# When layer 1's expert weights and row scatters are sent: 13 experts moved into attention rounds 7 and 8

## The reference

```python
x = x + L0_attn(layernorm(x))     # 16 heads of 16, RMS norm of q and k, rotary, causal softmax
x = x + L0_moe(layernorm(x))      # 16 experts, top 2, one shared expert
x = x + L1_attn(layernorm(x))     # 16 query heads, one key/value head, xpos rotary, causal softmax
x = x + L1_moe(layernorm(x))      # 32 experts in 8 groups, top 4 groups, top 8 experts, shared expert
```

## Time and profile before

| | us |
|---|---|
| median of 3 runs | 1161.76 |
| lowest and highest | 1159.61, 1175.99 |
| the profiled execution's own time | 1172.08 |
| its span | 1169.5 |
| TensorE busy, GpSimd busy in the span | 899.2 (77%), 621.2 (53%) |

### The profile page before, as it was taken

How to read it: one execution, slowest core, us unless ns; L and a number is a source line. 1 busy time by engine, 2 the same in 40 slices (tenths; PEclk the granted TensorE clock), 3 DMA queues, 4 the chain that set the end, 5 groups by cost and what they waited for, 6 DMA issues and landing times.

```text
span 1169.5 us, 22075 instructions
## 1 busy us (share of the span) xinstructions
PE 899.2 (77%) x5927; PEld 691.8 (59%) x5927; DVE 685.6 (59%) x2692; ACT 467.1 (40%) x1176; POOL 621.2 (53%) x870
## 2 busy tenths in 40 slices
PE   1687989878597992379987888856899999989900
PEld 1465667657355881256665565533688887778700
DVE  4678888865532554467687674352455544444568
ACT  2346666743112441257655443311344444444400
POOL 3646666523163652336558888755356655545500
PEclk9859999988798996559989576787999999999955
DMA  8500000000624543400002222566455655545287
GB/s 231 192 2 1 2 2 1 1 2 1 263 106 127 152 130 120 144 1 2 2 29 86 85 97 101 210 222 221 147 163 174 182 157 161 153 141 156 70 327 319
DMA packets 73093, 136.97 MB, mean 117 GB/s; under 512 B 13406, under 2 KB 51725, under 8 KB 70928
## 3 DMA queue, kind: packets, MB, share of 16 engines
q1 hardware_dynamic: 52144, 85.15, 22.8%
q0 software_dynamic: 17632, 46.73, 11.2%
q10 hardware_dynamic: 3200, 3.70, 0.9%
HBM read 79.15 MB, written 62.39 MB: 121 GB/s over the span
## 4 chain that ended last, share of the span: by engine, by line
PE 36%; DVE 9%; POOL 6%; issue 5%; ACT 2%; another core or an unknown queue 1%; DMA 1%; DVEq 0%; POOLq 0%; ACTq 0%; SPq 0%
PE s_psum L1996 12%; PE s_psum L2009 6%; PE s_psum L1988 3%; POOL rows L1553 3%; PE s_psum L1477 3%; PE s_psum L2004 2%; DVE a_masked L1074 2%; DVE f_rows L2096 2%; DVE f_xT L2096 2%; PE s_psum L549 1%; POOL a_probs L1414 1%; PE s_psum L1496 1%; PE s_psum L646 1%; PE s_psum L602 1%
## 5 line engine op out<-in xcount | busy, mean ns | idle before, releaser
L2106 POOL DMA_INDIRECT parts<-e_y,e_dest x206 | 202.7, 984 | 180.7 <-DVE e_y L2079 96.9
L1996 PE MATMUL s_psum<-wres,e_xT 128*128 x824 | 213.9, 382 | 1.8 <-ACT e_xT L2036 1.0
L1996 PEld LDWEIGHTS s_psum<-wres,e_xT 128*128 128x128 f32 x824 | 156.1, 191 | 26.1 <-issue 5.4
L1414 POOL TENSOR_SCALAR_AFFINE_SELECT a_probs<-a_probs 128x256 f32<-128x256 f32 x256 | 107.5, 444 | 117.6 <-ACT a_probs L870 116.8
L1553 POOL DMA_INDIRECT rows<-f_rows,f_place_at x128 | 125.2, 978 | 40.3 <-issue 31.7
L2009 PE MATMUL s_psum<-wres,e_hT 128*128 x412 | 125.3, 386 | 12.2 <-ACT e_hT L2046 11.6
L870 ACT ACTIVATE a_probs<-s_psum 128x768 f32<-128x768 f32 x128 | 104.6, 817 | 72.8 <-PE s_psum L629 68.2
L2041 ACT ACTIVATE e_act_out<-s_psum 128x128 f32<-128x128 f32 x206 | 57.1, 277 | 180.8 <-PE s_psum L1996 101.6
L2070 DVE TENSOR_TENSOR e_hid<-e_act_out,s_psum 128x128 f32<-128x128 f32 x206 | 59.0, 286 | 91.8 <-issue 42.6
L1074 DVE CUSTOM_DVE_ANT_0 a_masked<-s_psum,a_ahead 128x128 f32<-128x128 f32 (+1 forms) x256 | 76.1, 353 | 42.0 <-PE s_psum L605 39.1
L2079 DVE TENSOR_SCALAR e_y<-s_psum,e_xg 128x256 f32<-128x256 f32 x206 | 99.6, 484 | 0.7 <-issue 0.7
(11 more groups left out here) (297 smaller groups left out, 1993.4 us busy)
## 6 DMA issues: line engine op xcount, KB each, us to landing
e_xg<-rows SPq DMA_DIRECT2D x159, 160.0 KB
f_rows<-parts SPq DMA_DIRECT2D x8, 1024.0 KB, 7.2
f_xT<-parts SPq DMA_DIRECT2D x8, 1024.0 KB, 7.4
wres<-in_experts SPq DMA_DIRECT2D x21, 384.0 KB
e_xg<-rows SPq DMA_DIRECT2D x47, 144.0 KB
wres<-in_experts SPq DMA_DIRECT2D x4, 1536.0 KB
rows<-empty SPq DMA_DIRECT2D x1, 5120.0 KB, 24.1
e_yk<-parts SPq DMA_DIRECT2D x16, 256.0 KB, 2.9
```

The source lines that it names most:

```text
L1414: last = nc.gpsimd.affine_select(out=diagonal[:, :, a], in_=diagonal[:, :, a], compare_op=ALU.is_ge, fill=0.0, base=0, pattern=[[0, 2], [1 ...
L1996: last = nc.tensor.matmul(ps_u[b % 2][:, 0:2 * P], xT[b % 2][:, c * P:(c + 1) * P], wres[:, ds(e, 1), 2 * c * P:2 * (c + 1) * P].rearrange ...
L2106: nc.gpsimd.indirect_dma_start(out=parts[:, :], out_offset=bass.IndirectOffsetOnAxis(ap=dest[b % NY][:], axis=0), in_=y[b % NY][:], in_off ...
```

## The change

Experts 25 to 13 are sent in rounds 7 and 8: GpSimd's queue adds 1 to `paced` in each of the 13 steps from round 7 step 0 to round 8 step 4. The other 13 are sent one per four scatters from round 9 on (counts 76, 80, ...). SyncE waits for what still uses the memory: `group_ps` (the last stack transposed) ahead of the first, batch 5's shifted scores ahead of expert 18, batch 6's ahead of expert 15, batch 7's and the last maxima ahead of expert 12, the last placement ahead of expert 4. Experts 4 to 0 are single transfers too. In steps 0, 1 and 2 of round 9 and step 0 of round 10 there is one scatter instead of two, so 118 are sent in the loop and 10 in `finish`. Some buffers of the attention are allocated in another order, so that those in use longest lie under the lowest experts.

```diff
-PACED = 78
+STACK_EXPERTS, FIRST_QUERY_EXPERTS, SECOND_QUERY_EXPERTS = 19, 16, 13
+ROUND_STEPS = 13
+PACE = 4
...
+        pieces = NH // 2 + (NK // 2 if multi else 1)
+
+        def query_homes(i):
+            return (sb(f"qT{i}", [P, PAIRS, N], F32R), sb(f"kT{i}", [P, PAIRS if multi else 1, N], F32R))
+
+        ahead = sb("ahead", [P, TRI])
+        masked = wide("masked", [P, 2, 2, TRI])
+        max_stack = sb("max_stack", [P, TB, 2, 2 * NH, 2], F32R)
+        maxT = sb("maxT", [P, TRI], F32R)
+        pairs_by_age = {i: query_homes(i) for i in (1, 0, 2)}
+        qT, kT = ([pairs_by_age[i][n] for i in range(NQ)] for n in range(2))
...
-                sp.wait_ge(st_ps, PAIRS * B)
-                sp.wait_ge(max_done, PAIRS * B)
-                for n, e in enumerate(range(FREE_EXPERTS - 1, LAST_EXPERTS - 1, -1)):
+                sp.wait_ge(group_ps, NF * B)
+                for n, e in enumerate(range(FREE_EXPERTS - 1, -1, -1)):
+                    if e == STACK_EXPERTS - 1:
+                        sp.wait_ge(st_ps, PAIRS * (B - 2))
+                    if e == FIRST_QUERY_EXPERTS - 1:
+                        sp.wait_ge(st_ps, PAIRS * (B - 1))
+                    if e == SECOND_QUERY_EXPERTS - 1:
+                        sp.wait_ge(st_ps, PAIRS * B)
+                        sp.wait_ge(max_done, PAIRS * B)
+                    if e == LAST_EXPERTS - 1:
+                        sp.wait_ge(f_placed, B)
                     sp.wait_ge(front["paced"], n + 1)
                     sp.dma_start(env["wres"][:, e], front["w_experts"][e]).then_inc(front["wres_loaded"], 16)
...
                     if front is not None and (i, j) >= (4, 3):
-                        for _ in range(2):
+                        for _ in range(1 if (B + 1, 0) <= (i, j) <= (B + 1, 2) or (i, j) == (B + 2, 0) else 2):
...
-                            if scattered >= PACED and scattered % 2:
+                            scattered += 1
+                            if i > B and scattered % PACE == 0:
                                 passed(pool, front["paced"])
-                            scattered += 1
+                        if (B - 1, 0) <= (i, j) < (B - 1 + ROUND_STEPS // PAIRS, ROUND_STEPS % PAIRS):
+                            passed(pool, front["paced"])
...
-        @block.sync
-        def _(sp):
-            sp.wait_ge(placed, B)
-            sp.dma_start(wres[:, 0:LAST_EXPERTS], w_all[0:LAST_EXPERTS].rearrange("e p n -> p e n")
-                         ).then_inc(wres_loaded, 16)
...
-                if n % 2:
+                if n % PACE == PACE - 1:
                     passed(pool, front["paced"])
...
-                front["wres_loaded"], front["wres_count"] = make_sem("wres_loaded"), 16 * (2 + FREE_EXPERTS - LAST_EXPERTS)
+                front["wres_loaded"], front["wres_count"] = make_sem("wres_loaded"), 16 * (1 + FREE_EXPERTS)
```

More of the change, by code:

```diff
@@ L402, in attention @@
         rotated = wide("rotated", [P, TB, QK])
-        pieces = NH // 2 + (NK // 2 if multi else 1)
         stack = sb("stack", [P, TB, pieces * P], F32R)
[L405 to L411, removed]
         m_E = EXPERTS[0]
```

## The result

| | before | changed |
|---|---|---|
| median (runs) | 1167.96 (4) | 1180.13 (4) |
| lowest and highest | 1159.61, 1175.99 | 1177.92, 1185.54 |
| the profiled execution, its span | 1172.08, 1169.5 | 1177.92, 1175.5 |

A forecast was written before the change was run, and what follows sets the result against it. GpSimd was taken to pace rounds 7 and 8, gaps under full DMA rounds 9 to 11, TensorE's units the end. First block 8 us sooner, less 1 for the clock, gives 7 off 1161.76: 1155 us, range 1145 to 1168.

The forecast's parts named there:

- Step (1): Rounds 7 and 8: sending 13 experts there costs 1.5 us, within bounds of 0 and 5.
- Step (2): Rounds 9 to 11: fewer experts win back 7.9 of 9.9 us of gaps; statistics of batch 7 at 762.5.
- Step (3): Four scatters moved behind the norm of batch 7: from its statistics to SyncE's first block read stays 56.5 us.
- three conditions for the first block: Start of the expert blocks: all 128 scatters landed, all weights in, and TensorE through with its units.
- Step (4): TensorE behind batch 7's statistics: placement after 22.8 us instead of 31.5, at 785.3; units need 29, end 814, no longer last.
- Step (5): Buffer order, 26 single transfers instead of one of 5, and SyncE's extra waits: no cost.
- The clock's 1 us: First block on TensorE: matmuls after an idle stretch run 1.3 us too long at low clock; 1 taken off.
- A: Rival, whole kernel: no change, 1162 us, because the gaps are not the work of the transfers; chance 0.25.
- B: Rival, rounds 7 and 8: the transfers carry the gaps there, slower by 6 us, 1168; chance 0.13.
- C: Rival, rounds 7 to 11: all 9.9 us of gaps go, rounds 7 and 8 lose nothing, 1150 us; chance 0.12.

The follow-up runs named there:

- e10: The kernel before without the wait of the last 6 scatters for the fourth before them; 1140.56 us, ratio 1.0002.
- e1: The changed kernel with two scatters in every step, as before the change; 1180.27 us, ratio 1.0081.
- e6: The kernel before with the new buffer order and 13 experts sent in rounds 7 and 8; 1176.41 us, ratio 1.0112.
- e4: The changed kernel with 64 more instructions without effect on VectorE's queue ahead of layer 1's rounds; 1185.08 us, no ratio.
- e7: The changed kernel, with GpSimd waiting until all scatters have landed ahead of scatters 96, 104, 112 and 120; 1170.64 us, ratio 1.005.
- e13: The changed kernel, with GpSimd waiting until all scatters have landed ahead of scatters 104 and 120; 1177.63 us, ratio 1.004.
- e15: The changed kernel measured again without an edit, on a chip where the kernel before takes 1141.66 us; 1140.07 us, ratio 0.9988.
- e5: The kernel before with only the new order of the attention's buffers; 1162.93 us, ratio 1.0012.
- e11: The changed kernel measured again without an edit, on a chip where the kernel before takes 1171.96 us; 1179.67 us, ratio 1.0062.

## Why the prediction was wrong

**The step that failed: "I read these as engines that stand without instructions (or whose release is late) while the DMA engines are full."** Steps (2) and (4) built on it that emptying rounds 9 to 11 would give 7.9 us ahead of norm 7 and 8.7 behind it. In the changed kernel the unexplained parts of the longest gaps (10.0, 7.3 and 10.0 us) stand at DMA shares of 0.36, 0.53 and 0.56. In e10 the share is 0.84 to 0.93 and there is no gap. In e1 the share from norm 6 to norm 7 fell from 0.53 to 0.43 and the stretch kept its 29.9 us; in e6 the share from norm 7 to the placement fell from 0.63 to 0.33 and that stretch kept its 30.7. The same kernels (changed, early sending, no tail wait) have the gaps on the chips where before takes 1162 to 1172 us (three in the experiments) and don't on two where it takes 1141. So shown is: the gaps belong to the chip or what surrounds it there, and don't follow the DMA share. From norm 6 to the first turn they are worth 16.5 us (90.3 in before's profile, 73.8 in e10's). The blocks add 18.5 us (340.2 against 321.7), and there neither profile has an idle stretch of this kind; that part is unexplained.

**Step (1), the cost of rounds 7 and 8: right in its range.** Predicted 1.5 within 0 to 5. From norm 4 to norm 6 it was 53.7 us before and 52.7 after, of which 1.27 is the scatter put off; the transfers cost about 0.2 (e1, without that scatter, 0.2 too), with a DMA share of 0.65 and 0.53 for the predicted 0.63. The granted clock was 0.75 and 0.50 there, 0.75 and 0.57 before, and GpSimd had the pace in both.

**Step (2), statistics of batch 7 at 762.5: 767.12.** The 4.8 us of the slower stretch ahead of norm 4 account for it, 762.3 without them. That the sum comes out is luck: the same work took 25.7 to 28.2 us from norm 6 to norm 7 in e4, e7 and e13, not 23.4, and e1 shows that the early transfers alone did not shorten the stretch. What did stays open.

**Step (3), the row of scatters as the floor: right for the row.** 58.8 us were predicted from norm 7 to the first turn, 56.5 + 2.3. On the chip without gaps it was 57.5 (e15). In the first profiled execution it was 79.3, since TensorE's units, not the row, ended last: GpSimd was through at 819.78. The step's three conditions for the first block leave out VectorE's table, which held the read until 829.72.

**Step (4), "the placement comes at 785.3; the units need 29, end 814": failed most.** The placement came at 797.1, 30.0 us behind norm 7 instead of 22.8, and the units, with two gaps between them, took 49 us instead of 29, until 846. The prediction let gaps shrink only; it had one row against this, the 6.5 us of VectorE without a full DMA, called it "half explained" and went on.

**Step (5), places, single transfers, waits: right** for the places (e5). The clock's 1 us could not be told.

**The rivals.** A was right in that the gaps don't come with a full DMA and don't go with an emptier one. No change in the time is what e15 gave (0.9988); the first comparison and e11 did not. By "Runtime: NRT & Kernel Launch" of the Trainium skill (Instruction fetch mechanics) the crossing of a page is mostly hidden; the traces do not contradict it, since no packet of code moved in the changed kernel's unexplained 10 us ahead of the placement (e4). B had the sign right for the first comparison and the place wrong: 0.2 us was lost in rounds 7 and 8, and 20.2 behind the last placement. C's gain was seen on no chip.

**What stays open.** What makes the gaps on some chips: no row names a releaser, and what differs between the chips was not tried. Each chip's executions were made at one time, so chip and time are not told apart. Why early sending makes them cost more there (1.0112 alone, 1.0062 to 1.0148 in the changed kernel) when it costs nothing on a chip without them. And whether a pause of GpSimd's row shortens the gaps, as four profiles suggest, or the four came out so by chance.

## What to carry to other kernels

Idle time whose releaser the profile can't name is no evidence for contention, even where a full DMA stands beside it; before a change is built on it, run the unchanged kernel on several chips and see whether the idle time is there each time. Work that an engine is to do later pays only where that engine would otherwise wait for certain: here the four scatters put off turned into a wait ahead of norm 7 once the gaps were gone. And one comparison (1.0148) isn't the kernel's: on other occasions it was 1.006 and 0.999.

## What the runs showed of the hardware

The same kernel's median is 1141 us on two chips and 1162 to 1172 on three others, at the same granted clock (medians of 0.846 to 0.848 on all five). In the one kind VectorE and ScalarE start up to 10.0 us after their input is there (before 5.7 and 6.5; changed 10.0, 7.3 and 10.0; e4 10.0), in the six profiles of the other kind every idle stretch above 4.5 us of these two engines, from 735 us to the first turn, has TensorE as its releaser. The expert blocks show the difference too: 320 to 322 us against 329 to 341.

In the profiles of before and changed one packet of the two instruction queues moved in these parts, at 802.57 for 1.35 us.

Scatters on GpSimd follow each other every 1.265 us, at a DMA share of 0.93 (e10, 765 to 782 us) as at 0.43 (changed kernel, 800 to 831).

A releaser in brackets can be a transfer that landed long before (`rope_gamma` and `setup_tri` are sent at 2.1 and 2.3 us and are named at 810.21 and 820.78): with a long idle time such a name means unknown.
